# Norms taken chunk by chunk, beside the shared FFN and ahead of the second attention, with their roots as powers on GpSimd

## The reference

```python
x = x + 0.5 * _L0_ffn_ref(_layernorm(x), ...)    # routed0
x = x + _L0_attn_ref(_layernorm(x), ...)         # attention0
x = x + 0.5 * _L0_ffn_ref(_layernorm(x), ...)    # routed1, the same weights
x = x + 0.5 * _L1_ffn_ref(_layernorm(x), ...)    # gated0
x = x + _L1_attn_ref(_layernorm(x), ...)         # attention1
x = x + 0.5 * _L1_ffn_ref(_layernorm(x), ...)    # gated1, gated0's weights
```

## Time and profile before

| | us |
|---|---|
| median of three runs | 2306.8 |
| the runs | 2303.85, 2306.8, 2310.09 |
| the profiled execution | 2309.08 |
| its span in the trace | 2307.3 |

### The profile page before, as it was taken

How to read it: one execution, slowest core, us unless ns; L and a number is a source line. 1 busy time by engine, 2 the same in 40 slices (tenths; PEclk the granted TensorE clock), 3 DMA queues, 4 the chain that set the end, 5 groups by cost and what they waited for, 6 DMA issues and landing times. The chain is left out here.

```text
span 2307.3 us, 41892 instructions
## 1 busy us (share of the span) xinstructions
PE 2106.1 (91%) x14574; PEld 1824.1 (79%) x14574; DVE 1566.3 (68%) x3547; ACT 1384.6 (60%) x3606; POOL 783.3 (34%) x666
## 2 busy tenths in 40 slices
PE   5988979889899999999999999999999999999889
PEld 3666956658688888888888888888888888888778
DVE  6646766453587777777777777776777777777553
ACT  4224642244376767767677676776767667676543
POOL 0331003443134243432434334243342433324232
PEclk9999989999999999999999999999999999999999
DMA  5442044430100000000000000000000000000000
GB/s 192 106 104 45 1 152 101 106 80 1 35 3 13 6 4 10 3 9 10 3 6 4 13 6 4 10 4 8 2 12 6 3 10 4 8 1 2 22 30 28
DMA packets 50992, 67.33 MB, mean 29 GB/s; under 512 B 10081, under 2 KB 36961, under 8 KB 50657
## 3 DMA queue, kind: packets, MB, share of 16 engines
q1 hardware_dynamic: 40416, 51.80, 7.1%
q0 software_dynamic: 10368, 12.85, 3.3%
HBM read 49.15 MB, written 15.48 MB: 28 GB/s over the span
## 5 line engine op out<-in xcount | busy, mean ns | idle before, releaser
L1028 ACT ACTIVATE phase_pt_hi<-phase_ring 128x512 fp32r<-128x512 f32 (+3 forms) x680 | 346.0, 536 | 199.5 <-PE phase_ring L1013 196.5
L988 ACT ACTIVATE phase_p<-phase_scores,phase_bias 128x512 f32<-128x512 f32 (+3 forms) x680 | 417.2, 626 | 77.6 <-DVE phase_bias L976 76.0
L1033 DVE TENSOR_TENSOR phase_pt_lo<-phase_ring,phase_pt_hi 128x512 fp32r<-128x512 f32 (+3 forms) x680 | 394.3, 602 | 77.6 <-ACT phase_pt_hi L1028 77.4
L969 DVE TENSOR_REDUCE phase_peaks<-phase_scores 128x1 f32<-128x512 f32 (+3 forms) x680 | 395.3, 601 | 53.5 <-PE phase_scores L958 25.8
L1013 PE MATMUL phase_ring<-sb_ident,phase_p 128*128 128x128 f32 x2312 | 347.7, 274 | 39.0 <-DVE phase_pt_lo L1033 30.3
L122 PE MATMUL phase_y<-phase_pt_hi,phase_v_hi 128*128 128x256 f32 x1152 | 333.3, 289 | 0.0
L1013 PEld LDWEIGHTS phase_ring<-sb_ident,phase_p 128*128 128x128 f32 x2312 | 261.7, 141 | 82.7 <-issue 50.2
L124 PE MATMUL phase_y<-phase_pt_hi,phase_v_lo 128*128 128x256 f32 x1152 | 322.0, 280 | 0.0
L123 PE MATMUL phase_y<-phase_pt_lo,phase_v_hi 128*128 128x256 f32 x1152 | 321.6, 279 | 0.0
L1907 POOL TENSOR_TENSOR phase_straight<-phase_rot,phase_rope 64x512 f32<-64x512 f32 x128 | 163.6, 1278 | 378.7 <-ACT phase_rot L1785 378.7
L958 PE MATMUL phase_scores<-phase_k_hi,phase_q_hi 128*128 128x512 f32 (+2 forms) x640 | 252.6, 395 | 6.4 <-POOL phase_k_lo L1916 1.9
(11 more groups left out here) (249 smaller groups left out, 5180.1 us busy)
## 6 DMA issues: line engine op xcount, KB each, us to landing
phase_e_up<-expert_up SPq DMA_DIRECT2D x32, 352.0 KB, 3.6
phase_e_dn<-expert_down SPq DMA_DIRECT2D x32, 256.0 KB, 4.0
y_rows<-phase_zero SPq DMA_DIRECT2D x8, 512.0 KB, 9.4
xn_rows<-phase_ln_xn SPq DMA_DIRECT2D x8, 512.0 KB, 6.6
sb_x<-y_rows POOLq DMA_DIRECT2D x8, 512.0 KB, 10.9
phase_raw_qk<-qk SPq DMA_DIRECT2D x16, 256.0 KB, 2.6
phase_raw_up<-up SPq DMA_DIRECT2D x10, 256.0 KB, 4.4
sb_x<-x SPq DMA_DIRECT2D x4, 512.0 KB, 6.2
```

The lines of the kernel that those rows point to most:

```text
L969: dve.tensor_reduce(self.peaks[:, t % 2, c:c + 1], self.scores[:, at:at + self.width(t, c)], AX.X, ALU.max).then_inc(*self.peaked.one)
L988: act.activation(self.p[:, at:at + width], self.scores[:, at:at + width], ACT.Exp, bias=self.bias[:, t % 2:t % 2 + 1], accum_out=self.sums ...
L1028: act.activation(hi, value, ACT.Copy).then_inc(*self.t_hi.one)
L1033: dve.tensor_tensor(lo, value, as_f32(hi), ALU.subtract).then_inc(*self.t_lo.one)
```

## The change

**The norm by chunk.** Statistics, variance, power, inverse, rows and transposes are now steps of one chunk each. The root on ACT and the reciprocal are gone: POOL raises the variance to the power -0.5 (128x4 numbers, `pool_power`), and DVE corrects it in three small instructions and makes the shift in a fourth.

**Routed stages.** One step list now drives the norm, the logits and the shared FFN too. 20 of the 32 shared pieces stand before the first expert's rows, one right behind, and 11 over the experts. Of the 20, 12 stand before the rank: ten gate or up products and two halves of the sums. h and down have banks of their own, so h waits only until the one before has been copied. The idle matmuls before the first find are 4 instead of 14. SP loads chunk 0 of x first, then the constants, then the shared weights and the other chunks.

**Gated stages.** A table says behind which piece a step of the norm stands. gated0 also runs a second norm, for attention1: it measures, normalises and transposes chunks 0 to 2 as soon as their sums have been added, and loads the first head's weights and the rotary table. There the down of chunk 2 stands behind up(3, 1) instead of up(3, 5). The 10 and 4 idle matmuls ahead of up(0, 2) are gone, and gated1 begins with 14 instead of 25. Of the up weights, ACT rounds the last two behind the first silu in place of all before it.

**attention1** normalises chunk 3 alone. Its idle matmuls are 6 at the start and 6 before the first scores (before: 46, 14, 5 and 20).

**attention0** has its norm by the new steps and its bias added later on POOL; its idle matmuls are the same.

The core of the diff:

```diff
-    def act_root(self, act, g):
-        act.wait_ge(*self.varied[self.tag, g])
-        act.activation(self.root[:, self.tiles(g)], self.var[:, self.tiles(g)], ACT.Sqrt).then_inc(*self.rooted.one)
-
-    def dve_inverse(self, dve, g):
...
-        dve.reciprocal(rstd, root).then_inc(*self.step.one)
...
+    def pool_power(self, pool, c):
+
+        tiles = slice(4 * c, 4 * c + 4)
+        pool.wait_ge(*self.varied[self.tag, c])
+        pool.tensor_tensor(self.rstd[:, tiles], self.var[:, tiles], self.core.half[:], ALU.pow).then_inc(*self.powered.one)
+
+    def dve_inverse(self, dve, c):
...
+        dve.wait_ge(*self.powered[tag, c])
         dve.tensor_tensor(tmp, rstd, rstd, ALU.mult).then_inc(*self.step.one)
...
+        dve.scalar_tensor_tensor(tmp, tmp, -0.5, var, ALU.mult, ALU.mult).then_inc(*self.step.one)
...
+        dve.scalar_tensor_tensor(rstd, tmp, 1.5, rstd, ALU.add, ALU.mult).then_inc(*self.step.one)
```

The head of a routed stage's step list, where `fill(n)` puts in the next n shared pieces:

```diff
+        measure = lambda c: [("stats", c), ("power", c)]
+        scale = lambda c: [("inverse", c), ("rows", c)]
+        turn = lambda c: [("flip", c, 0), ("flip", c, 1)]
+        order += [*measure(0), ("feed weights", "gate"), ("feed weights", 0), *scale(0), ("feed weights", 1), *turn(0), *measure(1)]
+        fill(1)
+        order += [*scale(1), ("logits", 0)]
+        fill(1)
+        order += [*measure(2), *turn(1), ("back", 0), *scale(2)]
...
+        order += [("back", 3), ("best", 1), ("choose", 0)]
+        fill(1)
+        order.append(("choose", 1))
+        fill(1)
+        order.append(("choose", 2))
+        fill(2)
+        order += [("rank",), ("mark", 0), ("mark", 1)]
...
-                    pe.wait_ge(*self.weighed[tag, n - 1])
+                    pe.wait_ge(*self.h_copied[tag, n - 1])
```

The gated stages and attention1:

```diff
+    NEXT = {(1, 4): [("measure", 1, 0)], (1, 5): [("scale", 1, 0)], (2, 1): [("turn", 1, 0)], (2, 3): [("measure", 1, 1)],
+            (2, 5): [("scale", 1, 1)], (3, 0): [("turn", 1, 1)], (3, 2): [("measure", 1, 2)], (3, 4): [("scale", 1, 2)],
+            (3, 5): [("turn", 1, 2)]}
...
+            self.norms.append(Norm(core, sb, then, range(NCH - 1), after=lambda c: self.added[tag, c, 3], like=self.norm))
...
+        return I1M - 1 if c == NCH - 1 and not self.then else 1
...
-        self.core.keep_warm(pe, self.down_ps[:, 0, :], 55 if self.add_y else 25)
+        self.core.keep_warm(pe, bank, 55 if self.add_y else 14)
...
-                if c == 0 and m == 2:
-                    self.core.keep_warm(pe, self.down_ps[:, 0, :], 10 if self.add_y else 4)
...
-        core.keep_warm(pe, self.y[:], 46)
-        self.norm.pe_turn(pe, (0, 1))
-        core.keep_warm(pe, self.y[:], 14)
-        self.norm.pe_turn(pe, (2, 3))
-        core.keep_warm(pe, self.y[:], 5)
-        pe.wait_ge(*self.norm.ready)
+        core.keep_warm(pe, self.y[:], 6)
         for step in self.order:
             what, key = step[0], step[1:]
             if step == ("score", 0, 0, 0):
-                core.keep_warm(pe, self.y[:], 20)
+                core.keep_warm(pe, self.y[:], 6)
```

639 lines of the change are left out of this document (348 added, 291 removed).

## The result

The changed kernel takes 2317.96 us (median of six runs, 2317.11 to 2319.55); the kernel before, beside it on the same chip, took 2308.38 (2303.85 to 2310.53). The ratio is 1.0044, with a 95% interval of 1.0031 to 1.0057: slower by 0.3 to 0.6%, where 2289 was forecast.

A forecast was written before the change was run, and what follows sets the result against it. PE was taken to have room only at stage heads and between experts. The terms, -18.5 + 3.4 - 6.5 + 1 + 3 + 0 = -17.6 on 2309.08, gave 2291.5, less 2.3 for the median: 2289 us, range 2268 to 2303.

The forecast's parts named there:

- routed0 and routed1, "+1" and "+3": Routed stages: later rank, partly repaid by shorter expert pairs; routed0 +1 us (-8 to +10), routed1 +3 (-6 to +12).
- "+12.3": routed0: delay of the first scatter, at 92 us instead of 79.79, with the rank at 54 instead of 41.56.
- rival C: Heads of attention1, gated0 and both routed stages: fewer idle matmuls lower PE's clock, giving back 12 us, to 2301; chance 0.19.
- the pairs: Routed stages, behind the first scatter: two experts take 10.2 us instead of 12.7; four pairs give -10 per stage.
- gated0, "+3.4": gated0: transposes +3.1, wait before down(3) in the tail +3.3, earlier first silu at the head -3; +3.4 us (0 to +7).
- The power, "0.3": Norms: a power on GpSimd takes 0.3 us, as what it replaces; at 1.3, +1 each in gated1, gated0 and attention0.
- attention0, "0": attention0: first statistics wait for POOL's rows and the norm behind keeps its length; 0 us (-1 to +2).
- attention1, "-18.5": attention1's head: only chunk 3 is normalised there, so first scores come at 11.3 instead of 30.2 us; -18.5 (-14 to -22).
- gated1, "-6.5": gated1: fewer idle matmuls at the head -2.3, no wait before up(0, 2) -4.5, shifts +0.3; -6.5 us (-3 to -8).
- A: Routed stages gain too: rank at 47 rather than 54, pairs 9.3; routed0 -8, routed1 -6, total 2271 us; chance 0.26.
- B: Routed stages: rank becomes the bound and delays pass to the end, from +12 us per stage; 2313 to 2321; chance 0.08.
- 0.07 for slower: Whole kernel: chance given to a slower result, against 0.81 for faster and 0.12 for the same within 0.3%, 7 us.

The follow-up runs named there:

- warm_tail: The changed kernel with 10 idle matmuls ahead of gated0's last eight transposes and 6 behind them; 2314.32 us, ratio 1.0025.
- no_power: The changed kernel without the powers on POOL, the norm's scale made from a constant, so every norm has another scale; 2312.71 us, ratio 1.0016.
- pow_twice: The changed kernel with every power on POOL issued twice; 2327.07 us, ratio 1.0075.
- warm_gaps: The changed kernel with idle matmuls in PE's three longest waits of each routed stage; 2312.64 us, ratio 1.0016.
- choose_first: The changed kernel with shared pieces taken from between the steps of the expert choice, 8 instead of 12 before the rank; 2323.89 us, ratio 1.0054.
- two_and_two: Changed kernel with old routed stages and attention0; gated0 normalises chunks 0-1, attention1 2-3, down of chunk 2 behind the last up piece; 2291.43 us.
- rows_on_act: The changed kernel with all of chunk 3's rows in attention1 normalised on ACT, none on DVE; 2319.01 us, ratio 1.0051.

## Why the prediction was wrong

**routed0 and routed1, "+1" and "+3".** This step failed: +7.2 and +10.8, 14.0 of the 25.6 by which the profiled spans miss. Much of its working held. The rank came at 52.70 for 54, in routed1 48.9 us into the stage for 48.7 (351 less the old start at 302.3), and behind the pairs it was -0.8 and -1.1 for -1. What failed is the way from the rank to the first scatter, for which the forecast kept the 38 us of before: it took 43.5 and 43.1, so the first scatter of routed0 stands at 96.21 instead of 92 (+16.4 for the "+12.3"). I priced each wait by its length and put rival C's lower clock only at the heads, where it was cheap. It fell in the middle, behind waits that the new order makes. With them filled, the first scatter comes 3.2 earlier and the stage ends 3.3 earlier, and 5.3 of the medians come back. The remaining 2.1 of routed0's 5.3 us is, by the rows, waits of PE by their length: 1.74, 2.73 and 2.12, of which the idle matmuls fill the last two but leave them in place, against 0.86, 1.57, 0.66, 0.56 and 0.99 before.

The second term that failed is the pairs, -8.4 and -8.2 for -10. Four scatters of routed0 stand behind marks (last section) and take 4.4 us longer together, which is of the size that is missing; no run took the marks away. In routed1 I had also taken 3 where my own sum gave 4.

**gated0, "+3.4".** This failed too: +9.0. The tail's wait was there in sum (3.5 for 3.3), but that is partly luck: I had put all of it before down(3), released by POOL, where 1.06 stands, and 2.46 stand ahead of the transposes, for DVE's rows. The head was better than I took: up(0, 2) ends 5.3 us earlier in the stage, for 3. Missing were the lower clock in the last sums (10.6 us for the 72 matmuls of down(3), from 609.99 to 620.6, against 8.6 at 0.12 each) and in the transposes before them (0.8), and 3.0 more of PE's waits in the middle. Of these, 0.85 at 517.07 and 1.89 at 525.35 stand while gated0's own norm goes by chunk; only 1.32 at 582.34 stands ahead of transposes of the second norm. These terms with the 3.1 for the transposes give 7.1; about 2 us I can't place. warm_tail gives 3.6 back, leaving out the third chunk 7.5.

**The power, "0.3".** Mis-sized: 1.0. It was near the upper bound of 1.3 that I had named, for which I had allowed +1 in each of three stages, and by the medians it was worth 5.3 in all. Reading the price off DVE's small instruction was the mistake; POOL's row of 1.28 for 128 times the numbers was the nearer one.

**attention0, "0".** The profile has +3.1, above my upper end of 2, and the versions agree: 133.9 and more in ten profiles with the new norm, 130.8 to 132.6 in five with the old. The medians of the two versions that differ in it are 0.3 apart. Why the stage is longer stays open; the power bears on it, as no_power says, but pow_twice doesn't fit.

**attention1, "-18.5".** The mechanism was right, with -14.5. The scores were 1.8 late for the gap of 3.56 and the clock behind it; in the stretch from 621.4 to 650 the clock is 0.85. The remaining 2 us I can't place; the same code takes 1577.1 to 1579.2 us in the profiles of other versions, so they may be spread.

**gated1, "-6.5".** Right: -7.6, no gap before up(0, 2).

**The rivals.** A fell at the rank. B gave the right side, but not by its condition of +12 in each routed stage, and the pairs did take back 8.4 and 8.2 of the delay. Of its mechanism the last step holds: what is late at the first scatter is late at the end (3.6 and 3.6 in pow_twice, -3.2 and -3.3 in warm_gaps). C gave a real mechanism in another place. I took the two as alternatives, but an order in which handoffs wait for each other opens gaps, and most of the longer gaps lower the clock. So their prices add, and 0.07 for slower was too small.

## What to carry to other kernels

Price a wait of the matmul engine by its length and by a possible slow stretch behind it; where the wait can't go, idle matmuls in it bring back the second part. Independent work ahead of a serial chain delays the chain wherever the engines' queues are shared, but it also covers the chain's waits: taking it out brought the rank 4.5 us forward in choose_first and the first find 2.9 back. Before moving a step ahead, look which bank and which queue it shares with the step before it. When work goes ahead into an earlier stage, move as much as that stage hides, or fill the waits that it leaves: here two chunks, and three with the tail filled, came out equal.

## What the runs showed of the hardware

A power on GpSimd over 128x4 numbers takes 1.0 us, not much less than a product over 64x512 (1.28) with 128 times the numbers per row. How much of that is the operation and how much a fixed part, no run tells.

VectorE and GpSimd hold each other up. At the head of attention1, VectorE's two rows take 2.82 us beside two POOL operations:

```profile
627.88 2.82 DVE L239 TENSOR_SCALAR phase_p<-sb_x,phase_ln_mv,phase_ln_rstd 128x256 f32<-128x256 f32 x2
...
627.96 1.26 POOL L1996 TENSOR_TENSOR phase_straight<-phase_rot,sb_rope 64x512 f32<-64x512 f32 x1 [3.07 <-ACT phase_rot L1869]
629.30 1.25 POOL L1998 TENSOR_TENSOR phase_rot<-phase_straight,phase_crossed 64x512 f32<-64x512 f32 x1
```

In two_and_two the same instructions for chunk 2 take 2.82 as well, and those for chunk 3, with no POOL operation beside them, 0.73:

```profile
610.27 0.73 DVE L239 TENSOR_SCALAR phase_p<-sb_x,phase_ln_mv,phase_ln_rstd 128x256 f32<-128x256 f32 x2
```

The other way round, the scatter at 132.60 takes 3.10 instead of 1.6, because a mark has started just before it:

```profile
132.16 2.13 DVE L806 TENSOR_TENSOR phase_hot<-phase_slots,phase_rank_b 128x2048 bf16<-128x2048 bf16 x1
```

The mark ends at 134.29 and the scatter 1.4 later. Four scatters of routed0 start while a mark runs (100.69, 110.62, 122.32 and 132.60); they take 2.38 to 3.10, and each ends 1.40 to 1.42 us behind its mark. In the kernel before, the scatters last 1.6 throughout; there the mark starts behind the scatter, as at 80.30 behind the scatter of 79.79:

```profile
80.30 2.10 DVE L771 TENSOR_TENSOR phase_hot<-phase_slots,phase_rank_b 128x2048 bf16<-128x2048 bf16 x1
```

So which of the two starts first decides. The Trainium skill says in "SBUF — State Buffer", section "SBUF: two separate sides", that GpSimd and VectorE share a port pair as an exclusive lock for a whole instruction, where VectorE runs in a two-port mode, or has two inputs in SBUF while the GpSimd operation reads SBUF. The same section says that a DMA issued from GpSimd can't write its descriptors while VectorE runs in a two-port mode. The scatters behind a mark look like the second; but a mark is a product of two inputs in SBUF, which that passage does not name, so these rows go beyond it. The rows of attention1 look like the first, though VectorE's instruction is recorded 0.08 us before POOL's and is the one held up; in which mode it runs, no row shows. With these rows on ScalarE (rows_on_act), the two POOL operations take 1.26 each, as before; no run took the marks away from the scatters.
